# Value products and softmax sums in TensorE's column groups, and state-space angles as outer products

## The reference, cut to what matters

```
q = (query @ Wq + bq).reshape(B, Nq, 16, 8).transpose(0, 2, 1, 3)   # Nq = 512
k, v = the same of the 77 keys
attn = softmax(q @ k^T * SCALE0)
out = (attn @ v) @ Wo + bo
```

```
dt = jnp.exp(log_dt)
dtA = dt[:, None] * A                                # A complex
dC = C * (jnp.exp(dtA) - 1.0) / A
powers = jnp.exp(dtA[:, :, None] * jnp.arange(L))    # L = 512
K = 2.0 * jnp.einsum('dn,dnl->dl', dC, powers).real
```

## Time and profile before

| | us |
|---|---|
| median of 3 runs (lowest, highest) | 553.63 (551.61, 553.75) |
| profiled execution: time, span | 553.78, 552.0 |
| span: PE busy / DVE / ACT / POOL | 478.6 / 430.9 / 264.7 / 117.0 |
| mean granted TensorE clock | 0.933 |

### The profile page before, as it was taken

How to read it: one execution, slowest core, us unless ns; L and a number is a source line. 1 busy time by engine, 2 the same in 40 slices (tenths; PEclk the granted TensorE clock), 3 DMA queues, 4 the chain that set the end, 5 groups by cost and what they waited for, 6 DMA issues and landing times.

```text
span 552.0 us, 8986 instructions
## 1 busy us (share of the span) xinstructions
PE 478.6 (87%) x2883; PEld 370.6 (67%) x2883; DVE 430.9 (78%) x1781; ACT 264.7 (48%) x549; POOL 117.0 (21%) x198
## 2 busy tenths in 40 slices
PE   4386586799999999999999999999999999736971
PEld 3154234598975989848987985689878989514760
DVE  4378988885625787886797988899898789998667
ACT  4441466575456465564538456534474544411040
POOL 4522003122020031003015210310222331232021
PEclk9998595699999999999999999999999999956996
DMA  7900770002100004000003000000000000000000
GB/s 182 173 2 0 222 220 0 2 1 39 21 2 2 1 1 58 4 1 1 2 0 51 9 4 1 2 20 0 2 2 1 2 20 1 1 1 0 21 0 19
DMA packets 16176, 15.03 MB, mean 27 GB/s; under 512 B 1210, under 2 KB 14274, under 8 KB 16130
## 3 DMA queue, kind: packets, MB, share of 16 engines
q1 hardware_dynamic: 16130, 14.47, 11.7%
HBM read 9.15 MB, written 1.05 MB: 18 GB/s over the span
## 4 chain that ended last, share of the span: by engine, by line
PE 70%; DVE 22%; ACT 3%; issue 3%; POOL 2%; DMA 1%; DVEq 0%; POOLq 0%; ACTq 0%
PE moe_h L910 20%; PE moe_y L922 20%; PE side L865 5%; PE side L970 3%; PE side L980 2%; PE side L958 2%; DVE area L1394 2%; PE moe_h L932 2%; PE side L1001 2%; PE side L772 2%; DVE TOP L1384 1%; PE side L944 1%; PE side L989 1%; PE side L834 1%; PE side L1023 1%
## 5 line engine op out<-in xcount | busy, mean ns | idle before, releaser
L1132 ACT ACTIVATE HT<-moe_h,W 128x256 f32<-128x256 f32 x256 | 115.5, 473 | 104.0 <-PE moe_h L910 103.8
L910 PE MATMUL moe_h<-xnT_moe,W 128*128 128x256 f32 x512 | 138.0, 387 | 0.8 <-ACT HT L1132 0.7
L922 PEld LDWEIGHTS moe_y<-W,HT 128*128 128x128 f32 x1024 | 131.3, 192 | 8.8 <-issue 3.2
L922 PE MATMUL moe_y<-W,HT 128*128 128x128 f32 x1024 | 134.9, 276 | 0.0
L910 PEld LDWEIGHTS moe_h<-xnT_moe,W 128*128 128x128 f32 x512 | 88.3, 193 | 17.8 <-issue 7.2
L1370 DVE SCALAR_TENSOR_TENSOR X<-moe_y,RW,X 128x128 f32<-128x128 f32 x128 | 38.9, 346 | 8.1 <-PE moe_y L922 7.1
L865 PE MATMUL side<-PT,VP 128*72 128x512 f32 x80 | 43.1, 625 | 1.2 <-ACT PT L1112 1.2
L1394 DVE MATCH_REPLACE8 area<-TOP,area 128x77 f32<-128x77 f32 x192 | 40.9, 230 | 0.0
L932 PE MATMUL moe_h<-W 128*128 128x256 f32 x112 | 31.7, 436 | 0.0
L1384 DVE MAX8 TOP<-area 128x8 f32<-128x77 f32 x192 | 31.5, 230 | 0.0
L1704 POOL TENSOR_TENSOR area<-area 128x128 f32<-128x128 f32 x16 | 7.4, 463 | 110.3 <-ACT area L1155 110.3
(11 more groups left out here) (323 smaller groups left out, 851.8 us busy)
## 6 DMA issues: line engine op xcount, KB each, us to landing
W<-in_w SPq DMA_DIRECT2D x8, 512.0 KB, 7.7
QA<-Q SPq DMA_DIRECT2D x24, 128.0 KB, 4.4
X<-in_x SPq DMA_DIRECT2D x4, 256.0 KB, 6.5
KM<-area SPq DMA_DIRECT2D x6, 160.0 KB, 5.9
out_dram<-FO SPq DMA_DIRECT2D x3, 256.0 KB, 2.3
V<-in_vpack SPq DMA_DIRECT2D x1, 579.0 KB, 7.7
area<-in_r2pack SPq DMA_DIRECT2D x1, 576.0 KB, 8.0
area<-in_gpack SPq DMA_DIRECT2D x1, 576.0 KB, 8.5
```

The lines of the kernel that those rows point to most:

```text
L910: pe.matmul(moe_h[n % 2][:, 0:HS], W1[:, e, c * P:(c + 1) * P], xnT_moe[:, b % 2, h * HS:(h + 1) * HS], start=True, stop=True).then_inc(mo ...
L922: mm = pe.matmul(moe_y[m % 2][:, t * P:(t + 1) * P], HT[:, m % 2, c, t * P:(t + 1) * P], W2[:, e, c, :], start=(c == 0), stop=(c == HC - 1))
L1132: act.activation(HT[:, m % 2, c, :], moe_h[n % 2][:, 0:HS], ACT.Relu, bias=wc("b1")[:, e * HC + c:e * HC + c + 1]).then_inc(moe_h_ready, 1)
```

## The change

Attention: `VP` becomes 32 columns wide for each head pair, and is made once for all batches; the rest keys have their own matrices `VR`; `ZP` and `ZL` hold ones and zeros, so that a product with them gives each head's sum already spread over its 8 value rows. `PT` is five deep. A round multiplies four key tiles in the four column groups (0, 32, 64, 96) of the array, once by `ZP` into one bank and once by `VP` into a second (rounds 0 and 2), or the four 32-row pieces of the rest tile, each in its own 32 x 32 tile of the array on the diagonal (rounds 1 and 3). Both banks are held from the first round to the end. DVE reads them directly: reciprocal of the sums, times values. The two copies on ACT and the spread products are gone.

State space: `kgen_T` transposes four 128 x 128 tables once; angles and exponents are then outer products on PE with a 0/1-and-number matrix `ES` (a new input of 768 KB as loaded by four transfers), one 128 x 512 f32 product for `kgen_ang`, two for `kgen_rot`, three for `kgen_exp`, with 32 rows each. DVE does the rounding in four instructions of 128 x 512 each for `kgen_ang` and `kgen_rot`, reading PSUM; ACT takes exponentials straight from PSUM; `kgen_mul` moves to POOL. `kgen_base` 1 moves behind `kgen_rot` 0. `ORDER` is rewritten throughout.

```diff
@@ kernel_steps
-    out = [("kgen_base", 0, 0), ("kgen_base", 0, 1)]
+    out = [("kgen_base", 0, 0), ("kgen_T", 0, 0)]
     for dh in range(ND + 1):
         if dh < ND:
             out += [("kgen_ang", 0, dh), ("kgen_rot", 0, dh), ("kgen_sin", 0, dh)]
+        if dh == 0:
+            out.append(("kgen_base", 0, 1))
...
@@ ORDER (first and last line)
-S H2 S H5 K H2 K W2 F2 W2 F W2 F W6 F H3 K H K2 H2 W K H2 K H18 K8 H W K H2 K H2 K3 H E10 H E6 H2 K E2 K H C2 K E6 K
+H2 S2 W H6 K W5 F W F W F K F2 H3 K W K2 H W H K2 W4 H4 K H7 K H5 K5 H K3 H2 K3 H4 E2 K E2 H E5 K3 H E3 H C E3 K E
...
-Z
+T7 O T2 O T O T2 W T4 O T2 O2 W T O3 W8 O5 Z O Z3 O Z O Z O3 Z2 O Z W Z O Z2 O Z O Z W2
@@ FILLS
...
+         "kgen_T": 1, "kgen_ang": 1, "kgen_rot": 2, "kgen_exp": 3}
-NPT = 2
+NPT = NG
+ROUNDS = 4
@@ place_fills
-        if kind == "pv" and i % NG == 0:
-            held.add(take(("pv", b, 0, i // NG)))
+        if kind == "pv" and i == 0:
+            for g in range(2):
+                held.add(take(("pv", b, 0, g)))
@@ tensor
-                    mm = pe.matmul(dst[0:GROWS, :], VP[:, g, n, :], PT[:, i % NPT, :], start=(n == 0), stop=(n == NG - 1))
+                    for n in range(NM, NG) if rest else range(NM):
+                        emptied(pe, "score", b, NG * g + n)
+                    for n, vr in enumerate((ZL, VR)):
+                        dst = side[FILL[("pv", b, 0, n)][0]]
+                        for q in range(NM):
+                            c = slice(32 * q, 32 * q + 32)
+                            if rest:
+                                mm = pe.matmul(dst[c, :], vr[c, b, g, :] if n else vr[c, g, :], PT[c, NM, :], start=False, stop=(g == 1), tile_position=(32 * q, 32 * q))
+                            else:
+                                mm = pe.matmul(dst[c, :], VP[:, b, g, q, :] if n else ZP[:, g, :], PT[:, q, :], start=(g == 0), stop=False,
+                                               tile_position=(0, 32 * q))
-                        mm = pe.matmul(dst[64 * g:64 * g + 64, :], cc("spread")[64:GROWS, :], ZR[g][64:GROWS, :],
-                                       start=True, stop=True)
+                        pe.matmul(dst[:], UT[g, k * P:(k + 1) * P], ES[g, c * 512:(c + 1) * 512], start=True, stop=True,
+                                  tile_position=(DH * i, 0)).then_inc(full, 1)
@@ scalar
-                    act.activation(ZR[i][64:GROWS, :], src[64:GROWS, :], ACT.Copy).then_inc(rz_ready, 1)
-                    act.activation(OV[64 * i:64 * i + 64, :], src[0:64, :], ACT.Copy).then_inc(read, 1)
@@ vector
+                if kind == "attn_sum":
+                    src, read = filled(dve, "pv", b, 0, i)
+                    if i == 0:
+                        dve.reciprocal(OT[:], src[:]).then_inc(read, 1)
+                    else:
+                        emptied(dve, "pv", b, 0, 0)
+                        dve.tensor_tensor(OT[:], OT[:], src[:], ALU.mult).then_inc(read, 1)
-                    gelem(("y0", i), dve.tensor_tensor(G1a[:], u32, av, ALU.mult))
-                    gelem(("x1", i), dve.tensor_scalar(G1b[:], G1a[:], cc("cosoff"), None, ALU.add))
-                    gelem(("x2", i), dve.tensor_scalar(G2a[:, :, 0:CA], G1b[:], ROUND, ROUND, ALU.add, ALU.subtract))
-                    gelem(("x", i), dve.tensor_tensor(G1b[:], G1b[:], G2a[:, :, 0:CA], ALU.subtract))
...
+                    dve.tensor_scalar(G1b, src[:], cc("cosoff"), ROUND, ALU.add, ALU.add).then_inc(g_dve, 1)
+                    gelem(("y1", i), dve.tensor_scalar(G1c, src[:], cc("sinoff"), ROUND, ALU.add, ALU.add))
+                    dve.scalar_tensor_tensor(G1b, G1b, ROUND, src[:], ALU.subtract, ALU.subtract).then_inc(g_dve, 1)
+                    dve.scalar_tensor_tensor(G1c, G1c, ROUND, src[:], ALU.subtract, ALU.subtract).then_inc(read, 1)
@@ gpsimd
+                    gelem(("t1", i), pool.tensor_tensor(G1b[:], G1b[:], p1, ALU.mult))
+                    gelem(("t2", i), pool.tensor_tensor(G1c[:], G1c[:], p2, ALU.mult))
+                    gelem(("t3", i), pool.tensor_tensor(G1b[:], G1b[:], G1c[:], ALU.add))
...
+                    gelem(("t4", i), pool.tensor_tensor(G1d[:], G1d[:], G1b[:], ALU.mult))
+                    gelem(("tab", i), pool.tensor_tensor(G2c[:], G2c[:], G2b[:], ALU.mult))
```

More of the change, by code:

```diff
@@ L100, in head_steps @@
            ("q_split", b, 1)]
-    out += [("v_place", b, 0), ("x_bo", b, 0)]
+    out += ([("v_place", 0, 0)] if b == 0 else []) + [("x_bo", b, 0)]
     out += [("smax", b, t) for t in range(T)]
     out += [("smax_T", b, 0)]
[L104 to L111, removed]
+    for g in range(2):
+        for n in range(NG):
+            out.append(("score", b, g * NG + n))
+            if g == 1 and n == 0:
+                out.append(("pv", b, 1))
+        out.append(("pv", b, 2 * g))
+    out += [("pv", b, 3), ("attn_sum", b, 0), ("attn_sum", b, 1), ("o_proj", b, 0), ("ln_stats", b, "moe"), ("ln_apply", b, "moe"),
             ("norm_T", b, "moe"), ("router", b, 0), ("route_exp", b, 0), ("route_w", b, 0), ("w_T", b, 0),
@@ L719, in _ @@
             sp.dma_start(G, gpack).then_inc(v_in, 16)
+            for g in range(ND):
+                sp.dma_start(ES[DH * g:DH * (g + 1)], epack).then_inc(e_in, 16)
             sp.dma_start(B2[:], b2).then_inc(m_in, 16)
@@ L867, in _ @@
-                if kind == "attn_norm":
-                    dst, full = free_for(pe, kind, b, i)
-                    for g in range(2):
-                        pe.wait_ge(rz_ready, 2 * b + g + 1)
-                        mm = pe.matmul(dst[64 * g:64 * g + 64, :], cc("spread")[64:GROWS, :], ZR[g][64:GROWS, :],
-                                       start=True, stop=True)
-                    mm.then_inc(full, 1)
+                    g, rest = i // 2, i % 2
+                    if i == 0:
+                        for n in range(2):
+                            free_for(pe, "pv", b, 0, n)
+                        if b == 0:
+                            pe.wait_ge(v_placed, 1)
+                            emptied(pe, "setup_v", 0, 0, 4)
@@ L1184, in _ @@
                     act.wait_ge(g_dve, GD["x", i])
[L1185 to L1189 removed]
+                    act.activation(G1b[:], G1b[:], ACT.Sin, scale=-TWO_PI, bias=cc("cosrad")).then_inc(g_act, 1)
+                    emptied(act, "kgen_ang", 0, i)
+                    act.activation(G1c[:], G1c[:], ACT.Sin, scale=-TWO_PI, bias=cc("sinrad")).then_inc(g_act, 1)
+                    for n in range(2):
+                        emptied(act, "kgen_rot", 0, i, n)
+                    act.activation(G2b[:], G2b[:], ACT.Sin, scale=-TWO_PI, bias=cc("cosrad")).then_inc(g_act, 1)
                 if kind == "kgen_mm":
@@ new lines, in _ @@
+                if kind == "kgen_rot":
+                    G2b = G2b2[i % 2].rearrange("p d c -> p (d c)")
+                    if i >= 2:
+                        dve.wait_ge(g_pool, GP["tab", i - 2])
+                    for n in range(2):
+                        src, read = filled(dve, kind, b, i, n)
+                        dve.tensor_scalar(G2b[:, n * 512:(n + 1) * 512], src[:], cc("cosoff"), ROUND, ALU.add, ALU.add).then_inc(g_dve, 1)
+                    for n in range(2):
+                        src, read = bank(kind, b, i, n), side_read[FILL[(kind, b, i, n)][0]]
+                        dve.wait_ge(g_dve, GD["k%d" % n, i])
+                        dve.scalar_tensor_tensor(G2b[:, n * 512:(n + 1) * 512], G2b[:, n * 512:(n + 1) * 512], ROUND, src[:],
+                                                 ALU.subtract, ALU.subtract).then_inc(read, 1)
```

265 lines of the change are left out of this document (125 added, 140 removed).

## The result

The changed kernel takes 564.75 us (median of four runs, 563.41 to 566.48), the kernel before 553.69 beside it (551.61 to 554.29): ratio 1.0208, 95% interval 1.0169 to 1.0248. It is about 2% slower, on either side of 2% by the interval, and clearly not faster. The forecast was 550 and a range of 539 to 563, so both the direction and the range were wrong.

The account below looks back on a forecast made before the run. PE was taken to bound the middle (133 to 450 us), DVE and a chain of waits the start, chains the tail. From 553.8, start -5, middle +1.5 and tail 0 gave 550.3, stated as 550; range 539 to 563.

Parts of the forecast that it names:

- Sets of four at 1.00 (lower bound 0.86): Attention rounds on PE: a set of four f32 products takes 1.00 us, at least one product's 0.86.
- Rival (b): Value rounds: the four column groups do not overlap, a set costs 4 x 0.86, total 589 us; chance 0.12.
- 4.8 us of PE work less in the middle: Middle, attention on PE: 8.0 us a batch instead of 9.6, so 4.8 less over three batches.
- New waits of 2 us (0 to 6): Middle: PE waits for exponentials ahead of value rounds, some 0.7 us a batch, 2 in all, from 0 to 6.
- Five outer products among the experts, 4.3 us: Middle: five of the 24 outer products fall among expert products, 0.86 us each, adding 4.3 (from 3.5).
- The start, -5 us (-10 to +3): Up to the first expert product: it comes near 98 instead of 102.78, 5 us earlier; bounds 10 earlier, 3 later.
- Nineteen of the 24 are at places where PE waits anyway.: Start: 19 of 24 outer products stand ahead of the first expert product where PE waits, so only five were charged.
- POOL and the tail: POOL's 6.1 to 7 us a quarter is off the chain, nothing added for the norm; tail 0, between -3 and +2.
- The signs named beforehand: Wrong if sets 2 us or more, PE idle for banks, first expert product at 90 or after 103, PE below 98%.
- Rival (c): Held banks and late exponentials add waits, start gains nothing: 563 us, or 558 with half of it; chance 0.15.

Follow-up runs that it names:

- e1: Kernel before with the attention change alone, in the order of before, both sum steps right behind the last value round; ratio 1.0329.
- e9: Changed kernel, same results, outer products over all 128 rows, each quarter's tile having zeros in its other 96 rows; 554.86 us, ratio 1.0003.
- e10: e9 with some expert steps of batches 1 to 3 moved ahead of value rounds 0 and 2 and of o_proj; 558.18 us, ratio 1.0052.
- e11: Changed kernel with some expert steps of batches 1 to 3 moved ahead of value rounds 0 and 2 and of o_proj; 568.47 us, ratio 1.0235.
- e8: Changed kernel's order with the state-space change alone, the attention of before and its ten value products behind their scores; 566.46 us, ratio 1.0175.
- e7: Changed kernel with outer products over all 128 rows, summing all four quarters, so values differ and only time counts; 554.39 us, ratio 0.9978.
- e5: e1 with batch 0's sums placed behind kgen_ang 2 and the others where attn_norm stood; 560.25 us, ratio 1.0096.
- e2: Kernel before with the state-space change alone, in the order of before, the transposes ahead of setup_rhs; ratio 1.0385.
- e3: Kernel before with both the attention and state-space changes, in the order of steps of before; 580.96 us, ratio 1.0473.
- e6: e5 with the scores and value rounds of batches 2 and 3 spread over more expert steps; 599.32 us, ratio 1.0801.
- e12: e1 with batch 0's sums behind kgen_ang 2, its o_proj and norm ahead of kgen_rot 2, later state-space steps delayed; 568.81 us, ratio 1.0235.
- e13: e9 with batch 0's o_proj and norm ahead of kgen_ang 2, later state-space steps about 4 us of expert products later; 577.35 us, ratio 1.0409.
- e4: Changed kernel without warm steps 10 to 13 of batch 0, ahead of the scores; 564.84 us, ratio 1.0180.

## Why the prediction was wrong, step by step

- *Sets of four at 1.00 (lower bound 0.86).* Right: 0.93 to 0.96 (1.92 and 1.85 for two), in the rounds over full height and in those where the four tiles use rows of their own. Rival (b), 589, falls. The rule of the Trainium skill, page "TensorEngine Tiling (Array Packing)", Gotcha 1, that row tiles cannot access the same PSUM bank at once, does not agree with this trace: four 32x32 tiles write one bank in 0.93 us where one product alone takes 0.86. (The threshold put there was off: 0.3 us more a set would have made 559.9, 1.1% slower than before; 0.5% needs only 0.2.)
- *4.8 us of PE work less in the middle.* Right: 5.6 less in e1.
- *New waits of 2 us (0 to 6).* Mis-sized: 7.9 more idle time in e1, 7.2 more in e9. I priced one exponential at one place a round. The waits at the rounds alone are 3.1 (L887); the rest are mostly text steps and scores queued behind, 2.6 of it released by exponentials as well, and in e10 and e11 moving work ahead of the rounds did not give the time back.
- *Five outer products among the experts, 4.3 us.* They take 3.71 at 108.38 (two, at half clock) and 2.77 for the other three, 6.5 us. At full clock 5 x 0.88 is 4.4, so the price was right and the clock was not.
- *The start, -5 us (-10 to +3).* This is the step that failed. I had "PE's clock stays at its lower level for the rounds and outer products here, each 0.86 becoming 1.72" as a bound only and summed at 0.86. Measured +3.5. With full-height products (e9) the start is -3.3, and its steps come where I had put them: scores at 57.3 (forecast 57), the addition at 86.4 (87), the first expert product at 99.5 (98). So the chain was about right, and the clock is 6.8 of the 8.5 us by which I missed. Nor was it only the outer products: at half clock `kgen_mm` takes 3.52 where it takes 2.13 at full clock (118.71), and `o_proj` 2.01 where e9's takes 0.89.
- *"Nineteen of the 24 are at places where PE waits anyway."* Wrong: three stand directly ahead of the scores, and ten in the chain between the reciprocal and the transposes of the norm (L1051 x8, x4 and x8 from 84.51 to 102.80, two instructions each), where PE waits for nothing. At full clock it is half right: in e9 the four behind the reciprocal are on the chain, but then the chain goes over DVE and POOL from 85.77 to 97.23 and PE waits 1.69 and 1.79 us there.
- *What follows the start.* The other half of the failed step. No term of the sum had it: the lower clock went on for the first 11 us of expert products and cost the middle another 5.7 (376.1 against e9's 370.4).
- *POOL and the tail.* POOL's product was not in the chain. The norm beside it (four operations, 1.11 together at 197.65 where they run alone) takes 3.70 in the kernel before, 3.81 after and 4.90 in e9, so adding nothing was right here. The tail's -1.5 is within -3 to +2 by luck: before's profile has a tail of the shorter kind (83.8, clock 0.81), and the changed order's of that kind take 80.1 and 80.2 (e10, e8; also 0.81), 3.6 less.
- *The signs named beforehand.* Of those for "wrong", two came: the first expert product after 103, and PE below 98% between 133 and 450 (308.95 of 317, 97.5%).
- *Rival (c), 563 by new waits*, came out next to the measured time, but only half for its reason: its waits of 8 us about came true (7.2 to 7.9), the rest is the clock. That the number was near is luck.

The sum with the measured terms: start +3.5, sets -5.6, waits +7.9, outer products +4.4, half clock among the first expert products +5.7, tail -1.5: 14.4, of which 12.7 are in the spans; PE's work in the middle is 1 us lower in e9 than sets and outer products give (362.41 against 363.4), and the waits there are 7.2. So the half clock is the larger miss and the waits the second: with the clock back up (e9) the kernel is level with the one before, not 3.6 us faster as forecast, since the waits stand 5 to 6 above their term.

What stays open: whether some order of steps lets the middle keep the 5.6 us. None of those tried did, and no version with either half of the change clearly beat the kernel before (e7 and e9 equal it). What of "32 rows" leaves the clock low was not taken apart either: the rows used, or the tile position that goes with them.

## What to carry to other kernels

Price an operation on TensorE by its time at the clock it will get, and ask what it does to the clock of what follows. Here products of 32 rows kept PE busy all the time and ran, as did the first expert products behind them, at half clock, and padding them with rows of zeros won 10 us. Where an engine is saturated and its inputs come through a chain on others, work taken off it is only a gain if the chain has slack: read the distance from the first step of the chain to the step that needs its end, not the wait at one place. And a step that changes its engine (the sums, from ACT to DVE) must be placed anew in that engine's queue: 13.6 us of idle time in e1 came from a place that had been harmless.

## What the runs showed of the hardware

- The granted clock follows more than PE's busy share: 6.00 busy of 6.00 us with 32-row products at 0.50, 3.43 of 6.00 behind full-height ones at 1.00. With rows of zeros the clock was as high as with rows of data (0.92 and 0.90 from 60 to 103). Idle time counted as well: in e7 the clock fell to 0.50 behind 3.49 us without work. The Trainium skill, page "TensorE: Matmul & The Clock Gate", Part 1, says that the gate goes by how busy PE has been recently. By the busy time that the profile shows, these rows do not agree: the busier stretch is the one at half clock.
- A tail with the same steps has two lengths. With before's order there it takes 83.8 us in before's profile (clock 0.81) and 86.3 to 87.1 in those of e1, e2, e3, e5, e6 and e12 (0.76 to 0.79). With the changed order it takes 80.1 to 80.2 in e7, e8, e10 and e13 (0.81) and 81.9 to 82.4 in the changed kernel, e4, e9 and e11 (0.79). What decides it was not tried; a single span can be off by 2 to 3 us for it.
- In e5 a DVE operation of 1024 columns took 2.28 us (L1603 at 84.27) where the other three of that line take 0.75, while POOL's product of 1024 ran from 83.11 to 86.00 (2.89 us). That is the stall of the earlier trace rows at more than one microsecond: it ends 0.55 us behind POOL's. POOL's own operation was longer too (1.91 in the earlier trace rows), and it began while DVE's one before it was running (1.22 from 83.01).
